# Decoder layer in float32 parts: expert weight split moved from the first body to the second, and batch 0's q, k, v by full float32 products

## The reference

```python
x = x + attention(layernorm(x), Wq, Wk, Wv, Wo, rms_w)        # 16 heads, rotary, lightning attention in chunks of 128
x = x + cross(layernorm(x), ctx, W_k, b_k, gamma, beta)       # kv = ctx @ W_k.T + b_k; sim of p @ kv with kv; layernorm; softmax
x = x + experts(layernorm(x), Wr, We, be)                     # 8 experts of 256x256, the top 2 by the router, softmax of the two
```

## Time and profile before

| | |
|---|---|
| median of 3 runs | 180.37 us (179.76 to 180.98) |
| profiled execution, from its first to its last instruction | 178.7 us |
| TensorE busy | 152.3 us |
| VectorE busy | 126.4 us |
| ScalarE busy | 61.8 us |
| GpSimd busy | 35.9 us |
| mean granted TensorE clock | 0.971 |

### The profile page before, as it was taken

How to read it: one execution, slowest core, us unless ns; L and a number is a source line. 1 busy time by engine, 2 the same in 40 slices (tenths; PEclk the granted TensorE clock), 3 DMA queues, 4 the chain that set the end, 5 groups by cost and what they waited for, 6 DMA issues and landing times.

```text
span 178.7 us, 3036 instructions
## 1 busy us (share of the span) xinstructions
PE 152.3 (85%) x983; PEld 106.6 (60%) x983; DVE 126.4 (71%) x396; ACT 61.8 (35%) x171; POOL 35.9 (20%) x54
## 2 busy tenths in 40 slices
PE   0399964797997999999959999999599889998991
PEld 0267433573662678867626888677258757745880
DVE  0633599647487995975789959757899565877762
ACT  3346880103487132054751320547613220311110
POOL 3104163013161002222410013125100113010020
PEclk9999996569999999999999999999999999999999
DMA  5999200000200000000004000000010000001001
GB/s 173 290 360 340 57 0 4 0 0 2 69 10 0 0 4 0 0 2 0 0 4 132 0 0 0 0 0 0 0 59 0 4 2 0 0 0 59 4 0 59
DMA packets 7930, 7.29 MB, mean 41 GB/s; under 512 B 2264, under 2 KB 7664, under 8 KB 7792
## 3 DMA queue, kind: packets, MB, share of 16 engines
q1 hardware_dynamic: 7424, 6.79, 12.1%
q10 hardware_dynamic: 496, 0.37, 0.7%
HBM read 6.11 MB, written 1.05 MB: 40 GB/s over the span
## 4 chain that ended last, share of the span: by engine, by line
PE 43%; DVE 33%; issue 7%; ACT 6%; DVEq 5%; POOL 3%; DMA 2%; POOLq 0%
PE bank L784 15%; PE ebank L784 11%; DVE probs L613 9%; PE bank L894 4%; POOL rs L325 3%; DVE b_e_parts L738 3%; DVE stats L519 2%; ACT qx L425 2%; PE ebank L792 2%; DMA xin<-in_x 2%; DVE norm L530 2%; DVEq L520 2%; PE bank L799 2%; DVE acc L557 2%; PE bank L890 1%
## 5 line engine op out<-in xcount | busy, mean ns | idle before, releaser
L613 DVE TENSOR_TENSOR probs<-bank,dec 128x512 f32<-128x512 f32 x32 | 19.8, 683 | 1.9 <-PE bank L852 1.9
L852 PE MATMUL bank<-qx,kT 64*128 64x512 f32 x64 | 18.4, 625 | 0.7 <-ACT kv L480 0.7
L325 POOL TENSOR_TENSOR rs<-ve,nhalf 128x2 f32<-128x2 f32 x16 | 11.4, 711 | 36.6 <-DVE ve L524 36.5
L877 PE MATMUL bank<-probs,vpad 128*32 128x128 f32 x256 | 10.8, 293 | 4.1 <-DVE probs L613 4.1
L799 PE MATMUL bank<-cst,norm 128*128 128x128 f32 x36 | 6.4, 301 | 9.1 <-DVE norm L530 9.1
L784 PE MATMUL ebank<-w_e_hi,h3T_hi 128*128 128x512 f32 x40 | 13.3, 413 | 0.0
L557 DVE SCALAR_TENSOR_TENSOR acc<-ebank,gate,acc 128x256 f32<-128x256 f32 x26 | 11.3, 477 | 2.5 <-PE ebank L784 2.3
L425 ACT ACTIVATE qx<-bank,cst 128x256 f32<-128x256 f32 x32 | 12.6, 489 | 0.0
L557 DVE SCALAR_TENSOR_TENSOR acc<-bank,gate,acc 128x256 f32<-128x256 f32 x22 | 9.3, 478 | 4.5 <-PE bank L784 3.0
L784 PE MATMUL ebank<-w_e_hi,h3T_lo 128*128 128x512 f32 x40 | 12.5, 393 | 0.0
L784 PE MATMUL ebank<-w_e_lo,h3T_hi 128*128 128x512 f32 x40 | 12.4, 392 | 0.0
(11 more groups left out here) (135 smaller groups left out, 332.8 us busy)
## 6 DMA issues: line engine op xcount, KB each, us to landing
w_e<-in_L_ffn_We SPq DMA_DIRECT2D x2, 1024.0 KB, 10.8
xin<-in_x SPq DMA_DIRECT2D x4, 256.0 KB, 3.6
dec<-in_decay SPq DMA_DIRECT2D x1, 1024.0 KB, 7.9
out<-outb SPq DMA_DIRECT2D x8, 128.0 KB, 1.7
cst<-in_consts ACTq DMA_DIRECT2D x1, 282.0 KB, 3.6
w_qkv<-in_L_attn_Wq SPq DMA_DIRECT2D x1, 256.0 KB, 4.2
w_qkv<-in_L_attn_Wk SPq DMA_DIRECT2D x1, 256.0 KB, 4.6
w_qkv<-in_L_attn_Wv SPq DMA_DIRECT2D x1, 256.0 KB, 4.9
```

The costliest lines, as they stand in the source:

```text
L325: nc.gpsimd.tensor_tensor(dst[:], src[:], nhalf[:], ALU.pow).then_inc(done, 1)
L613: nc.vector.tensor_tensor(probs[:, t, 4 * n:4 * n + 4, :], bank[2 + n][:].rearrange("p (h n) -> p h n", h=4), dec[:, 4 * n:4 * n + 4, :], ...
L852: pe.matmul(bank[2 + n][:], kT[rows, t, g, :], qx[rows, t, g, :, :], start=True, stop=True).then_inc(s_sc_ps, 1)
L877: mm = pe.matmul(bank[t][32 * q:32 * q + 32, g * P:(g + 1) * P], vpad[:, t, h, :], probs[:, t, h, :], start=(par == 0), stop=(par == 1 and ...
```

## The change

It has five parts.

1. The split of the expert weights leaves body 0 but for ScalarE's two casts, of which the second now comes behind `attention_out(1)`. GpSimd's subtraction and VectorE's 128x2048 one are gone. In body 1 VectorE makes all low parts in four pairs of 128x512 pieces (`low_experts(0)` to `low_experts(3)`, columns of two experts each, both chunks). TensorE waits for all of them at the start of the bodies with experts, and no longer ahead of the router product, which waits for the router's part alone.
2. In body 0, q, k, v are full float32 products of `h1T_full` (the transposed norm, copied as float32) and the unsplit weights (`full_product`, `qkv_first`). The low part of h1T is not made there. The weights' own split stays, for the later bodies.
3. Constant products: one of 512 and one of 256 columns ahead of the first transposes, in place of the one ahead of `qkv(0)`; one of 512 ahead of `state_product`; one of 256 between `attend(0)` and `attend(1)`.
4. The scaling of `w_o` moves from behind the second tile's score decay to ahead of the first tile's.
5. The bias and router low parts move behind `decay_scores(1)`.

```diff
@@ GpSimd, body
-                if front and not back:
-                    pool.wait_ge(s_hi, 2)
-                    nc.gpsimd.tensor_tensor(w_e_s[1][:, 0], w_e[:, 0], w_e_s[0][:, 0].bitcast(F32),
-                                            ALU.subtract).then_inc(s_lo, 1)
@@ ScalarE, body
+                def high_experts(c):
+                    act.wait_ge(s_we[c], 16)
+                    act.copy(w_e_s[0][:, c], w_e[:, c]).then_inc(s_hi, 1)
...
-                    transposed(0, i, bank[0:2], h1T[0])
+                    transposed(0, i, bank[0:2], h1T[0] if back else h1T_full)
...
-                    for c in range(KC):
-                        act.wait_ge(s_we[c], 16)
-                        act.copy(w_e_s[0][:, c], w_e[:, c]).then_inc(s_hi, 1)
+                    high_experts(0)
...
                     attention_out(1)
+                if front and not back:
+                    high_experts(1)
@@ VectorE, body
+                def low_experts(q):
+                    if not (front and back) or experts:
+                        return
+                    cols = slice(2 * q * D, 2 * (q + 1) * D)
+                    dve.wait_ge(s_hi, 1 + KC)
+                    for c in range(KC):
+                        nc.vector.tensor_tensor(w_e_s[1][:, c, cols], w_e[:, c, cols], w_e_s[0][:, c, cols].bitcast(F32),
+                                                ALU.subtract).then_inc(s_lo, 1)
...
                     ln_apply(0, xin, i)
+                low_experts(0)
...
-                if front:
+                if front and back:
                     low_parts(0, i, bank[0:2], h1T)
...
                     ln_stats(3, lambda t: sim_banks[t][:, 0:T], s_sv)
+                    low_experts(1)
...
                     ln_stats(2, lambda t: x2[:, t, :], s_var[2])
+                low_experts(2)
...
                                                 ALU.mult, ALU.add).then_inc(s_rms_var, 1)
+                    low_experts(3)
                     dve.wait_ge(s_rms_rstd, i + 1)
@@ TensorE, body
+                def full_product(dst, cols, w_cols):
+                    for c in range(KC):
+                        mm = pe.matmul(dst, h1T_full[:, c, cols], w_qkv[:, c, w_cols], start=(c == 0), stop=(c == KC - 1))
+                    return mm
+                def qkv_first(t):
+                    pe.wait_ge(s_nT[0], t + 1)
+                    cols = slice(t * P, (t + 1) * P)
+                    if t == 0:
+                        pe.wait_ge(s_wqkv[0], 16)
+                        pe.wait_ge(s_wqkv[1], 16)
+                    full_product(bank[t][:], cols, slice(0, 2 * D))
+                    if t == 0:
+                        pe.wait_ge(s_wqkv[2], 16)
+                    full_product(bank[2 + t][:, 0:D], cols, slice(2 * D, 3 * D)).then_inc(s_qkv_ps, 1)
...
+                if first:
+                    keep_clock(1, ebank[0])
+                    keep_clock(1, ebank[0], 256)
...
+                if experts:
+                    pe.wait_ge(s_lo, 1 + KC * E // 2)
...
-                if first:
-                    keep_clock(1, ebank[0])
...
+                if first:
+                    keep_clock(1, ebank[0])
                 if front:
                     state_product()
                     scores(1)
                 if back:
-                    pe.wait_ge(s_lo, 1 + KC)
+                    pe.wait_ge(s_lo, 1)
...
                     attend(0)
+                    if first:
+                        keep_clock(1, ebank[0], 256)
                     attend(1)
```

More of the change, by code:

```diff
@@ L147, in decoder_layer @@
         h1T = [sb(f"h1T_{n}", [P, KC, T], F32R) for n in ("hi", "lo")]
+        h1T_full = sb("h1T_full", [P, KC, T])
         qk = sb("qk", [P, TILES, 2 * D])
@@ L717, in body @@
                     if not back:
+                        dve.wait_ge(s_wo, 16 * (1 + KC))
+                        for c in range(KC):
+                            nc.vector.tensor_scalar(w_o[:, c, :], w_o[:, c, :], rms_col[:, c:c + 1], None,
+                                                    ALU.mult).then_inc(s_wo_scaled, 1)
                         dve.wait_ge(s_dec, 16)
@@ L734, in body @@
                                             ALU.mult).then_inc(s_st, 1)
+                if front:
+                    decay_scores(1)
+                if back:
+                    route()
                 if front and not back:
@@ L740, in body @@
                     nc.vector.tensor_tensor(w_r_s[:, :, 1, :], w_r[:], w_r_s[:, :, 0, :].bitcast(F32), ALU.subtract).then_inc(s_lo, 1)
-                if front:
-                    decay_scores(1)
-                if back:
-                    route()
-                if front and not back:
-                    dve.wait_ge(s_hi, 3)
-                    nc.vector.tensor_tensor(w_e_s[1][:, 1], w_e[:, 1], w_e_s[0][:, 1].bitcast(F32),
-                                            ALU.subtract).then_inc(s_lo, 1)
-                    dve.wait_ge(s_wo, 16 * (1 + KC))
-                    for c in range(KC):
-                        nc.vector.tensor_scalar(w_o[:, c, :], w_o[:, c, :], rms_col[:, c:c + 1], None,
-                                                ALU.mult).then_inc(s_wo_scaled, 1)
                     dve.wait_ge(s_gb, 32)
@@ L786, in split_product, with keep_clock @@
                 return mm
-            def keep_clock(n, dst):
+            def keep_clock(n, dst, cols=512):
                 for _ in range(n):
-                    pe.matmul(dst[:], ident, cst[:, 0:512], start=True, stop=True)
+                    pe.matmul(dst[:, 0:cols], ident, cst[:, 0:cols], start=True, stop=True)
             def transposes(n, b, banks):
@@ L827, in expert_unit @@
                                   slice(2 * q * D, 2 * (q + 1) * D)).then_inc(s_ex, 1)
-                def qkv(t):
-                    pe.wait_ge(s_nT_lo[0], TILES * i + t + 1)
+                def full_product(dst, cols, w_cols):
+                    for c in range(KC):
+                        mm = pe.matmul(dst, h1T_full[:, c, cols], w_qkv[:, c, w_cols], start=(c == 0), stop=(c == KC - 1))
[10 more added lines that the diff above has]
+                    full_product(bank[2 + t][:, 0:D], cols, slice(2 * D, 3 * D)).then_inc(s_qkv_ps, 1)
+                def qkv(t):
+                    if first:
+                        return qkv_first(t)
+                    if t == 0:
+                        pe.wait_ge(s_wqkv_lo, 3)
+                    pe.wait_ge(s_nT_lo[0], TILES * (i - 1) + t + 1)
                     cols = slice(t * P, (t + 1) * P)
                     split_product(bank[t][:], h1T, w_qkv_s, cols, slice(0, 2 * D))
-                    if first and t == 0:
-                        pe.wait_ge(s_wqkv_lo, 3)
                     if t == 0:
@@ L948, in body @@
                 if front:
-                    if first:
-                        pe.wait_ge(s_wqkv_lo, 2)
                     qkv(0)
                     if first:
+                        pe.wait_ge(s_c, 1)
                         pe.wait_ge(s_wctxT, TILES)
```

## The result

The changed kernel took 174.44 us in the median of four executions (174.34 to 175.66), the kernel before 180.25 beside it: a ratio of 0.9692, 95% interval 0.9657 to 0.9727. The forecast was 174.0. The profiled execution's span is 172.3 us against 178.7. Ratios leave out executions over 1.5% above a kernel's fastest, while medians are of all: that leaves out two executions each of front_only and front_again and one each of split_only and tail_keep4.

What follows compares the result with a forecast made beforehand. The prediction took a chain of waits passing between TensorE and VectorE as the bound. From a 178.7 us span, 9.4 off in body 0 and 3.0 on in body 1 gave 172.3, with 1.67 around it 174.0 us; range 171.2 to 177.0.

Steps and rivals of the forecast that it cites:

- (a): Start of body 0: q, k, v end at 15.2 us, 1.0 us gained, bounds plus 1.5 and minus 0.5.
- (b): Body 0: bias and router pieces hold up the next score quads for 4.85 us, all of which goes.
- not the limit, by some 0.3 us: Body 0: TensorE gives scores(1) quads from 22.5 us, VectorE wants them from 22.8, so they don't bind.
- needs two SBUF operands: Body 0: GpSimd's long instruction with two SBUF operands keeps out VectorE's bias piece of the same kind, which took 4.62 us.
- (c): Tail of body 0, attention to x1: x1 at 29.6 us against 39.03, the tail giving 3.5 of 9.4 us.
- has no gap over 1 us left: Tail of body 0: TensorE has no such gap, so its clock was taken to stay at 1.00.
- is paid twice: Body 0: TensorE idles from 25.4 to 29.4 us, and its clock falls to 0.50 until 38 us.
- (d): Body 1: the first pair of low parts costs nothing, the three others 1.0 us each, 3.0 in all.
- The rule of full exclusion: Body 1: VectorE and GpSimd shut each other out, each pair costs 1.2 us, 3.7 in all; 174.7 us, chance 0.2.
- the fall in the tail: Tail of body 0: the clock goes to 0.50 as before, about 2.3 us more; 176.3 us, chance 0.08.
- the slower one: Body 1: three longer waits send the clock to 0.50 into the experts, up to 15 us; 189 us, chance 0.02.
- the bias piece is slow by itself: Body 0: its cast and 32 lanes make it slow; same gain, or near 179 if score quads slow; chance 0.03.

Runs made afterwards that it cites:

- front_only: The kernel before with part 2 and the two constant products ahead of the transposes alone; 177.79 us, ratio 0.9848.
- front_again: The kernel before with part 2 and the two constant products ahead of the transposes, run once more for its profile; 177.57 us, ratio 0.9829.
- split_only: The kernel before with part 1 of the change alone, the expert split moved to body 1; 174.81 us, ratio 0.9687.
- tail_keep4: The changed kernel with low parts as single pieces in body 0's tail and body 1, and four constant products instead of three starting body 1; 173.57 us, ratio 0.9612.
- old_front: The changed kernel with the front of before: split products of batch 0, the constant product ahead of them, h1T's low part; 175.17 us, ratio 0.9735.
- no_late_consts: The changed kernel without the constant products ahead of state_product and between the attends; 173.05 us, ratio 0.9590.
- one_input: The kernel before with the bias and router low parts written by pieces that read one SBUF tensor; 180.03 us, ratio 0.9991.
- tail_pieces: The changed kernel with chunk 0's four low-part pieces in body 0's tail and one chunk 1 piece at each of body 1's four places; 174.54 us, ratio 0.9687.
- stall_filled: The kernel before with four 512-column constant products between attend(0) and attend(1), in TensorE's idle time; 179.99 us, ratio 0.9973.
- placed: The changed kernel without late constant products, three early ones on zeros, four starting body 1, low parts as single pieces in waits without roots; 171.59 us, ratio 0.9496.

## Why the prediction was right, step by step

The time was right to 0.4 us, and the forecast change of the span, 6.4 us, is the measured one. But it was 9.4 - 3.0, and measured were 7.98 - 1.58. The mechanism was right (the stall, its end, the pairs that cost less than it), and the size of both terms was too large. That the two errors cancel is luck.

(a) The front: forecast 1.0 gained, q, k, v ending at 15.2. In the profile it was 16.12, a gain of 0.13. The step that failed is that the first tile would run at full speed: its eight matmuls took 3.35 us where I had 2.75, and the second tile's 2.78. They also began at 9.37 and not 9.1. TensorE came to full speed in the first tile although it had been at work from 4.65 us. In the profiles with this front the end lay between 14.8 and 16.1; the forecast is inside, the bounds (-0.5 to +1.5) held. In the medians (old_front) the front is worth 0.8 us.

(b) The stall: right in its cause, its size (4.85 us) and in that it goes entirely. What I said comes next was wrong: I found scores(1) "not the limit, by some 0.3 us". I had VectorE's first quad of it 0.5 us behind its start (22.0 to 22.5); it came 1.09 us behind (22.81 to 23.90), as it had for scores(0) before (19.52 to 20.68). So VectorE waited 0.20 us, and the chain above runs on TensorE through both new constant products (1.06 and 0.63 us). By no_late_consts they cost 0.8 us in the profiles and 1.4 in the medians. And that the stall needs two SBUF operands was wrong (one_input).

(c) The tail: from the attends' start to x1 I forecast 5.9 us, and it took 5.94 (24.72 to 30.66). The start was at 24.72 and not 23.7: 0.92 of this is what (a) fell short by; the constant product ahead of state_product was already in that sum. And the step "x1 at 29.6 against 39.03" set the first tile's start against the second's; by the statistics' start the same forecast is a gain of 9.0. The rest of the way to 7.98 is the later start. That TensorE "has no gap over 1 us left" was wrong: the gap ahead of body 1's transposes is 1.28 us. It cost nothing in this profile; in split_only and tail_pieces the way from pair 0 (or its piece) to the next one was 4.9 and 4.6 us instead of 3.5. And that the stall "is paid twice" held for the profile I built on, with some 2.3 us for the clock, while filling the stall gave 0.6 in the medians (stall_filled).

(d) The pairs: pair 0 free, as forecast. For the others I took 1.0 us each, between 0.5 (side by side) and 1.2 (in turns). Pairs 1 and 2 cost 0.4 each, below my lower end: on the chain a pair is 1.19 us, against a wait of 0.80. Pair 3 I had misread: the 0.80 us ahead of x1 ended with TensorE's projection and not with a root (the bracket in the earlier trace rows names bank L894). It reached the chain only by TensorE's wait for the last low parts, 0.24 us ahead of the first expert product. In all 0.96, and 0.27 for the first units, against 3.0; with the 0.35 untraced 1.58. This term was the worst sized. The rule of full exclusion, a rival at 174.7 us with 0.2, came out nearer the measured time (174.44) than my own 174.0 but is not what happens: neither do pair and root add up nor do the roots delay the pieces.

Of the rivals with the clock, the fall in the tail did not come (clock 1.00 to 45 us), and the slower one needed a clock that stays down; where it fell in body 1, it was back after 3 us. That the bias piece is slow by itself is excluded by 0.42 us in the changed kernel.

## What to carry to other kernels

Ahead of moving work off an engine because that engine looks busy, look for a short instruction with a long duration: it shows who holds what it needs, and the cure is to move the long one. Work that is put in a wait for a small GpSimd instruction lengthens that instruction, even if it fits the wait; in waits for TensorE or ScalarE the same pieces cost 0.3 us in all (placed). Price a half-speed clock from several executions, since when it rises and falls differs between them, and fill TensorE's gaps only where nothing on the chain stands behind the filling.

## What the runs showed that I had not expected

- A 128x2 root on GpSimd took 1.06 us instead of 0.69 when one 0.64 us subtraction of VectorE began 0.17 us ahead of it, and 0.80 with a 0.38 us piece; the VectorE pieces kept their length in both.
- A VectorE piece with one SBUF operand waited 4.49 us for GpSimd's subtraction, like one with two.
- Three constant products on a tile of zeros, from 1.8 us on, had TensorE at full speed at 7.58 us, where the transposes took 0.67 us, though it had computed nothing but zeros. That the earlier start did it isn't shown by one profile: with the two products from 4.57 us on they took 0.69 in tail_keep4 and 1.09 in the changed kernel.
- A gap of 1.28 us (split_only) and of 1.65 us (tail_pieces) was followed by a clock of 0.50 for about 3 us, 1.2 and 1.8 us behind the gap's end, while the same gap of 1.28 us in the profiles of the changed kernel, no_late_consts and old_front was not.
- A kernel's executions can fall into two groups 3 us apart (some 177.5 and 180.6 us, front_only); one profile of each differs by 3.5 us in its span, of which 3.2 lie in body 0, where TensorE ran at another clock.
